# Graph attention and mixture-of-experts kernel: attention weights in a PSUM bank, two banks for the aggregates, the mask product in two halves

## The chip, the cores and the metric

The kernel runs on one core of a Trainium2 chip. The metric is device time in microseconds (us) of one execution; several executions give a median. The engines of the core are named as in the profile: PE is TensorE (matrix products; PEld are its weight loads), DVE is VectorE, ACT is ScalarE, POOL is GpSimd, SP is SyncE, which issues transfers.

## The reference

3125 nodes with 256 features, 50000 edges (src, dst, type), three layers of graph attention, then a feed-forward network of eight experts with the best two chosen per node. The part that the change touches is the message passing of a layer:

```
Q, K, V = (h @ W.T + b).reshape(-1, H, DH)  for Wq, Wk, Wv        # H = 4 heads, DH = 64
scores  = einsum('ehd,egd->ehg', Q[src], K[tgt]) / sqrt(DH)       # per edge: 4 x 4
attn    = softmax(scores, axis=-1)
msg     = einsum('ehg,egd->ehd', attn, V[tgt]) + Ee[et]
m       = segment_sum(msg @ Wo.T + bo, src)
h       = relu(layer_norm(h + m))
```

The scores of an edge are 4 by 4: each head of the source's query against each head of the target's key. The softmax runs over the four key heads, and the sum collects per source node.

## The kernel before

**Stages.** A sorting stage (to some 380 us) orders the edges by source window and scatters their records to memory; the input stage computes the first queries, keys and values; then come three times an edge phase (some 780 us each) and a node phase (some 120 us); at the end the experts.

**Edge phase.** Nodes stand in windows of 16. Edges are sorted so that a tile of 128 edges belongs to one window. Two tiles are a pair; a layer has 294 pairs (EP). A turn of the loop has 12 pairs (PAIRS): 24 full turns and one of 6 pairs per layer. The engines work side by side, each with its own program, and only semaphores order them:

- POOL gathers for each tile the 128 rows of keys and values of the edges' targets, 2 KB each, by one indirect transfer (L573, `arena<-kv_d,gidx`), two per pair, 588 per layer. The buffer `kv` holds 24 tiles, a whole turn; before POOL gathers a pair anew it waits for that pair's `agg_done` of the turn before.
- PE does for pair p, in this order: the transposes of the keys of pair p + 1 (`keys`, L1545, four) into bank 3 or 4; the aggregate of pair p - 6 (`aggregate`, L1570; LAG = 6), values times spread weights, into bank 5, 6 or 7; then `scores` of pair p into bank 0, 1 or 2. These begin with the mask product (L1553): the one-hot of the edge's node in its window, `oh[..., 1, :]`, in bf16, times a constant `maskc`, 512 columns at once, which lifts the 16 columns of the edge's own node above the others. Then follow the products of transposed keys and block-diagonal queries (L1560), which add to it. In the program an fp32 product is one call; the trace counts two instructions for it (x8 for four).
- ACT copies the transposed keys to SBUF (L1306, `kT_ready`), lays out the queries of the next pair (L1301, L1302), and copies the aggregate of pair p - 7 to `stage` in two copies (L1313, `staged`); every fourth pair it takes the exponential (L1321).
- DVE takes the largest over the 16 nodes of the window (`best`, L828), which leaves 4 by 4 scores; every fourth pair the softmax of eight tiles at once: L834 and L838, then L843, L845 and L847, which writes the normalized weights `at_s` (128x128 for eight tiles); per pair `spread` (L857): `at_s` times the one-hot `oh[..., 0, :]`, giving `att`, 128x512; and `add` (L875, two per pair), which adds `stage` to the sums of the window.
- SP loads the one-hots `oh`, one transfer for four pairs.

**Waits around the change.** `aggregate` waits for `att_ready` (the spread of its pair) and for `staged`, so that its bank has been copied out. `scores` waits for `score_read` (DVE has read the bank's earlier scores), every fourth pair for the transfer of `oh`, and, behind the mask product, for `kT_ready`. The counts of `staged` start from LAG + 3, which gives the three banks: the aggregate of a pair waits for the staging of the pair three before.

The spread, with its two operands, is

```
dve.tensor_tensor(att[...], at_s[...] (each weight for 16 nodes), oh[:, t // TG, 0, ...] (each one-hot for 16 weights), ALU.mult)
```

Of the kernel before, what the change touches and what calls it, by code (L numbers as in the profile page):

```python
# [22 lines left out]
P = 128  # L23
N, D, H, DH, E, L = 3125, 256, 4, 64, 50000, 3
# [17 lines left out]
UB = 4  # L42
# [4 lines left out]
NTURN = -(-EB // TURN)  # L47
LASTB = EB - (NTURN - 1) * TURN
TILES = TURN * UB
PAIRS = TILES // 2  # L50
# [3 lines left out]
LAG = 6  # L54
AL = LAG + 1
GP = 4
# [30 lines left out]
def build(nc, A, out):  # L87
    ctx = ExitStack()
    with ctx:
        def sb(name, shape, dt=F32):  # L90
            return ctx.enter_context(nc.sbuf_tensor(name, shape, dt))
# [15 lines left out]
        ident = sb("ident", [P, P])  # L107
# [4 lines left out]
        maskc = sb("maskc", [P, TG, DH], BF16)  # L112
# [11 lines left out]
        kv = arena[:, 0:n_kv].rearrange("p (b u n) -> p b u n", b=TURN, u=UB)  # L124
# [38 lines left out]
        ex = sb("ex", [P, 2 * GP, H, H])  # L163
        sm = sb("sm", [P, 2 * GP, H])
        rc = sb("rc", [P, 2 * GP, H])
        at_s = sb("at_s", [P, 2 * GP, H, H])
        att = sb("att", [P, 2, UB, W, H, H])

        early = arena[:, 0:n_kv]
# [46 lines left out]
        oh = sb("oh", [P, TILES // TG, 2, P], BF16)  # L216
# [98 lines left out]

        bank = [ctx.enter_context(nc.psum_tensor(f"bank{i}", [P, 512], F32)) for i in range(8)]
        bank_b = [b[:, :].bitcast(BF16) for b in bank]

        names = ("const_landed idx_landed start_ready spare wincode_ready counted place_ready perm_built perm_used "
                 "perm_done cnt_saved rec_ready wincnt_done base_ready ohwin_ready rank_ready rank_read "  # L320
# [11 lines left out]
        S = namedtuple("Semaphores", names)(*[sem(n) for n in names])  # L332
# [3 lines left out]
        gathered = [sem(f"gathered{k}") for k in range(TILES)]  # L336
        oh_landed = [sem(f"oh_landed{c}") for c in range(TILES // TG)]
# [203 lines left out]
        @block.gpsimd  # L541
        def _(pool):
            for s, k in ((S.hT_done, G), (S.q_ready, G), (S.kvp_ready, 2),
                         (S.agg_done, PAIRS), (S.score_read, 4), (S.att_ready, LAG), (S.staged, LAG + 3), (S.chain_b, AL + 2), (S.chain_a, AL)):
                pool.sem_inc(s, k)
            pool.sem_inc(S.m_y_ready, 2)
            for j in range(G):
# [4 lines left out]
            for e in range(EC):  # L552
                if e % CH == 0:
                    pool.wait_ge(S.slot_ready, e // CH + 1)
                r = P if e < EF else ER
# [123 lines left out]
        def _(dve):  # L679
# [144 lines left out]
            def e_phase(l):  # L824
# [41 lines left out]

                def add(p, u, at, q):
                    if u == 0:
                        dve.wait_ge(S.staged, at[q + 2])
                        dve.wait_ge(S.chain_b, at[q + 1])  # L870
                    else:
                        dve.wait_ge(S.chain_a, at[q])
                    w = dve.snap(wreg[2 * p + u], min_val=0, max_val=NW - 1)
                    a = acc[:, ds(w, 1), :].squeeze(1)
                    dve.tensor_tensor(a, stage[:, p % 3, u, :], a, ALU.add).then_inc(S.chain_a if u == 0 else S.chain_b, 1)  # L875
# [349 lines left out]
        def _(act):  # L1225
# [67 lines left out]
            def e_phase(l):  # L1293
# [15 lines left out]
                def sums_out(p, done, added):  # L1309
                    act.wait_ge(S.agg_done, done)  # L1310
                    act.wait_ge(S.chain_b, added)
                    for r in range(2):
                        ins = act.activation(  # L1313
                            stage[r * DH:(r + 1) * DH, p % 3].rearrange("p u (h s) -> p u h s", h=H),
                            bank[5 + p % 3][r * DH:(r + 1) * DH, 0:2 * P].rearrange("p (u g s h) -> p g u h s", u=2, g=2, h=H)[:, r],
                            ACT.Copy)
                    ins.then_inc(S.staged, 1)

# [136 lines left out]
        def _(pe):  # L1455
# [81 lines left out]
                pe.wait_ge(S.ee_ready, l + 1)  # L1537

            def e_phase(l):
                def keys(p, landed):  # L1540
                    for t in (2 * p, 2 * p + 1):
                        pe.wait_ge(gathered[t], landed)
                        for c in range(KC):
                            o = (t % 2) * D + c * P
                            ins = pe.transpose(bank[3 + p % 2][:, o:o + P], kv[:, t // UB, t % UB, c * P:(c + 1) * P], ident[:, :])  # L1545
                    ins.then_inc(S.kT_done, 1)

                def scores(p, at, here):
                    bk = bank[p % 3]
                    pe.wait_ge(S.score_read, at[p + 1])  # L1550
                    if p % 4 == 0:
                        pe.wait_ge(oh_landed[p // 4], here[p // 4 // 2])
                    mm(bk[:, :], oh[:, p // 4, 1, :],  # L1553
                       maskc[:, 2 * (p % 4):2 * (p % 4) + 2, :].unsqueeze(2).to_broadcast([P, 2, H, DH]),
                       start=True, stop=False, skip_group_check=True)
                    pe.wait_ge(S.kT_ready, at[p])
                    for u in range(2):
                        for c in range(KC):
                            o = u * D + c * P
                            ins = mm(bk[:, o:o + P], kt_s[:, p % 2, u, c, :], qbd[:, p % 4, u, :],  # L1560
                                     start=False, stop=(c == KC - 1), skip_group_check=True)
                    ins.then_inc(S.score_done, 1)

                def aggregate(p, ready):
                    pe.wait_ge(S.att_ready, ready)
                    pe.wait_ge(S.staged, ready)
                    for t in (2 * p, 2 * p + 1):
                        b, u, o = t // UB, t % UB, t % 2 * P
                        for g in range(0, H, 2):
                            ins = mm(bank[5 + p % 3][:, o:o + P], kv[:, b, u, D + g * DH:D + (g + 2) * DH],  # L1570
                                     att[:, b % 2, u, :, g:g + 2, :].rearrange("p s g h -> p g s h"),
                                     start=(g == 0), stop=(g == H - 2), skip_group_check=True)
                    ins.then_inc(S.agg_done, 1)

                def turn(i, first, last):
                    pairs = LASTP if last else PAIRS
                    at = [pe.snap(l * EP + i * PAIRS + p + 1) for p in range(pairs + 1)]
                    here = [pe.snap((l * (NTURN - h) + i + 1) * 16) for h in range(2)]
                    ahead = pe.snap((l * NTURN + i + 2) * 16)
                    for p in range(pairs):  # L1580
                        if p + 1 < pairs:
                            keys(p + 1, here[(p + 1) * 2 // PAIRS])
                        elif not last:
                            keys(0, ahead)
                        if p >= LAG or not first:
                            aggregate((p - LAG) % PAIRS, at[p])
                        scores(p, at, here)

                keys(0, pe.snap((l * NTURN + 1) * 16))
                turn(0, True, False)  # L1590
                with nc.tensor.Fori(1, NTURN - 1) as i:
                    turn(i, False, False)
                turn(NTURN - 1, False, True)
                for p in range(LAG):
                    aggregate((LASTP - LAG + p) % PAIRS, pe.snap(l * EP + EP + p + 1))
# [294 lines left out]
```

## Time and profile before

| | |
|---|---|
| time, median of 3 runs | 3674.46 us (3667.35 to 3678.6) |
| span of the profiled execution | 3674.3 us |
| PE busy | 3426.8 us, 93% of the span |
| ACT busy | 2698.7 us, 73% |
| DVE busy | 2458.4 us, 67% |
| POOL busy | 2459.9 us, 67% |
| mean granted clock of PE | 0.974 |
| edge phases, first to last gather | 516.1 to 1283, 1414.2 to 2180.7, 2311.8 to 3078.9 us |

The span is that of one execution on the chip; it lies on the median of the timed ones. The shares are averages over stages that have different limits. A busy PE is not a PE at its peak, since the ends of its products are modelled; what one product costs in a row of them is read from the starts. The pauses between two gathers of POOL count as idle, though POOL waits for nothing in them that the profile shows ("issue").

### The profile page before, as it was taken

The page shows a single profiled execution, that of the slowest core. Times are in us where ns is not written, and L with a number is a line of the kernel's source. Part 1 is how long each engine was busy: PE and PEld are TensorE (multiplying, and loading weights), DVE is VectorE, ACT ScalarE, POOL GpSimd, SP SyncE. Part 2 cuts the span into 40 slices and gives each one's busy share as a digit, 9 for nine tenths or more (in the row PEclk, how much of TensorE's full clock was granted, in tenths as well). Part 3 has the DMA queues.
Part 4 walks back from the last instruction along what each step waited for, and adds up shares of the span by engine and source line. Part 5 has one row for each costly group of instructions (what it writes and reads, how often), then busy time and mean ns, then how long its engine had stood idle before and what let it go on. Part 6 is the DMA issues. An engine that isn't in the chain of part 4 may idle for free.

```text
span 3674.3 us, 87831 instructions
## 1 busy us (share of the span) xinstructions
PE 3426.8 (93%) x25408; PEld 2968.4 (81%) x25409; DVE 2458.4 (67%) x6794; ACT 2698.7 (73%) x8426; POOL 2459.9 (67%) x2552
## 2 busy tenths in 40 slices
PE   6888879999999998999999999899999998969998
PEld 2444559999999966999999986799999997759998
DVE  7888447777777765777777775577777777931111
ACT  4999678888888856888888876788888885424443
POOL 3777127777777775777777776677777776725443
PEclk9999879999999999999999999999999999979999
DMA  2000257777777726777777753677777776446664
GB/s 80 1 1 1 90 207 205 208 208 207 207 208 206 206 94 193 205 208 207 207 206 207 208 160 115 206 206 206 209 206 207 206 207 195 155 155 182 185 176 120
DMA packets 264903, 630.75 MB, mean 172 GB/s; under 512 B 56095, under 2 KB 128726, under 8 KB 256471
## 3 DMA queue, kind: packets, MB, share of 16 engines
q0 software_dynamic: 161376, 477.59, 46.5%
q1 hardware_dynamic: 103431, 152.05, 12.4%
q8 instruction: 39, 0.64, 0.1%
q14 instruction: 57, 0.47, 0.0%
HBM read 577.72 MB, written 52.04 MB: 171 GB/s over the span
## 4 chain that ended last, share of the span: by engine, by line
PE 47%; POOL 18%; issue 17%; DMA 10%; DVE 5%; ACT 2%; DVEq 0%; POOLq 0%; SPq 0%; ACTq 0%
POOL arena L573 12%; PE bank L1570 10%; DMA arena<-kv_d,gidx 9%; PE bank L1560 8%; POOL rec_d L557 6%; PE bank L1761 5%; PE bank L1545 5%; PE bank L1773 5%; PE bank L1529 4%; PE bank L1523 2%; PE bank L1553 2%; PE bank L1605 2%; PE bank L1611 1%; DVE att L857 1%; PE bank L1683 1%
## 5 line engine op out<-in xcount | busy, mean ns | idle before, releaser
L573 POOL DMA_INDIRECT arena<-kv_d,gidx x1764 | 1763.6, 1000 | 729.1 <-issue 529.8
L1570 PE MATMUL bank<-att,arena 128*128 128x128 f32 x7056 | 946.3, 278 | 22.9 <-DVE att L857 19.4
L1560 PEld LDWEIGHTS bank<-qbd,kt_s 128*128 128x128 f32 x7056 | 932.2, 193 | 33.2
L1560 PE MATMUL bank<-qbd,kt_s 128*128 128x128 f32 x7056 | 934.8, 276 | 0.0
L1570 PEld LDWEIGHTS bank<-att,arena 128*128 128x128 f32 x7056 | 862.4, 193 | 42.0 <-DVE att L857 39.9
L828 DVE TENSOR_REDUCE sc<-bank 128x32 f32<-128x512 f32 x882 | 607.6, 689 | 313.7 <-PE bank L1560 301.7
L1306 ACT ACTIVATE kt_s<-bank 128x512 f32<-128x512 f32 x882 | 526.6, 597 | 253.3 <-PE bank L1545 239.8
L1545 PE MATMUL bank<-ident,arena 128*128 128x128 f32 x3528 | 623.4, 283 | 61.7 <-DMA arena<-kv_d,gidx 49.4
L857 DVE TENSOR_TENSOR att<-at_s,oh 128x512 f32<-128x512 f32 x882 | 608.3, 690 | 25.9
L1545 PEld LDWEIGHTS bank<-ident,arena 128*128 128x128 f32 x3528 | 407.9, 142 | 163.9 <-DMA arena<-kv_d,gidx 124.2
L875 DVE TENSOR_TENSOR arena<-stage,arena 128x64 f32 x1764 | 398.2, 226 | 196.1 <-DVE arena L875 112.4
L1301 ACT ACTIVATE qbd<-arena 64x64 f32 x1764 | 441.8, 250 | 92.6 <-issue 82.3
L1313 ACT ACTIVATE stage<-bank 64x128 f32<-64x128 f32 x1764 | 478.7, 271 | 34.6 <-DVE arena L875 10.3
L1302 ACT ACTIVATE qbd<-arena 64x64 f32 x1764 | 449.6, 255 | 20.5
L557 POOL DMA_INDIRECT rec_d<-arena x241 | 251.1, 1042 | 133.6 <-issue 78.3
L1553 PE MATMUL bank<-maskc,oh 128*128 128x512 bf16 x882 | 336.2, 381 | 0.0
L1213 DVE TENSOR_TENSOR arena<-bank,arena 128x256 f32<-128x256 f32 x56 | 23.8, 425 | 356.3 <-PE bank L1773 356.3
L658 POOL DMA_INDIRECT out<-arena,row_at x56 | 90.8, 1622 | 187.6 <-DVE arena L1217 184.6
L1761 PE MATMUL bank<-xT,arena 128*128 128x128 f32 x1792 | 210.6, 276 | 0.0
L1761 PEld LDWEIGHTS bank<-xT,arena 128*128 128x128 f32 x1792 | 205.8, 193 | 0.4 <-ACT xT L1436 0.4
L1428 ACT ACTIVATE arena<-bank,arena 128x128 f32<-128x128 f32 x448 | 121.6, 384 | 113.5 <-PE bank L1761 113.3
L1773 PE MATMUL bank<-arena 128*128 x896 | 202.6, 380 | 0.0
(246 smaller groups left out, 3999.8 us busy)
## 6 DMA issues: line engine op xcount, KB each, us to landing
arena<-in_pack SPq DMA_DIRECT2D x56, 1030.0 KB, 5.1
arena<-kv_d,gidx POOLq DMA_INDIRECT x1764, 3.7
oh<-oh_d SPq DMA_DIRECT2D x222, 64.0 KB
kv_d<-arena SPq DMA_DIRECT2D x50, 256.0 KB, 2.0
xin<-hid_d SPq DMA_DIRECT2D x75, 128.0 KB, 2.2
arena<-in_w SPq DMA_DIRECT2D x8, 1024.0 KB, 7.2
kv_d<-arena SPq DMA_DIRECT2D x5, 1280.0 KB, 5.1
hid_d<-arena SPq DMA_DIRECT2D x50, 128.0 KB, 2.0
```

The costliest lines, as they stand in the source:

```text
L557: pool.indirect_dma_start(rec_d, bass.IndirectOffsetOnAxis(slot_all[0:r, e:e + 1], 0), pay[0:r, e:e + 1], None,).then_inc(S.scattered, 16)
L573: pool.indirect_dma_start(kv[:, t // UB, t % UB, :], None, kv_d, bass.IndirectOffsetOnAxis(gidx[:, h, t - h * HT:t - h * HT + 1], 0),).the ...
L828: dve.tensor_reduce(sc[:, 2 * m:2 * m + 2], bank[q % 3][:, :].rearrange("p (t g s h) -> p t g h s", t=2, g=H, s=W), AX.X, ALU.max).then_in ...
L857: dve.tensor_tensor(att[:, b, u:u + 2].rearrange("p t s g h -> p t s (g h)"), at_s[:, 2 * m:2 * m + 2].rearrange("p t g h -> p t (g h)").u ...
L1301: act.activation(qbd[0:DH, p % 4, u, 0:64], q, ACT.Copy)
L1302: act.activation(qbd[DH:P, p % 4, u, 64:128], q, ACT.Copy)
L1306: act.activation(kt_s[:, p % 2], bank[3 + p % 2][:, :].rearrange("p (u c n) -> p u c n", u=2, n=P), ACT.Copy).then_inc(S.kT_ready, 1)
L1313: ins = act.activation(stage[r * DH:(r + 1) * DH, p % 3].rearrange("p u (h s) -> p u h s", h=H), bank[5 + p % 3][r * DH:(r + 1) * DH, 0:2 ...
L1545: ins = pe.transpose(bank[3 + p % 2][:, o:o + P], kv[:, t // UB, t % UB, c * P:(c + 1) * P], ident[:, :])
L1560: ins = mm(bk[:, o:o + P], kt_s[:, p % 2, u, c, :], qbd[:, p % 4, u, :], start=False, stop=(c == KC - 1), skip_group_check=True)
L1570: ins = mm(bank[5 + p % 3][:, o:o + P], kv[:, b, u, D + g * DH:D + (g + 2) * DH], att[:, b % 2, u, :, g:g + 2, :].rearrange("p s g h -> p ...
L1761: ins = mm(bank[1 + 2 * (p % 2) + h // 4][:, (h % 4) * P:(h % 4 + 1) * P], w1s[:, p, c * HID + h * P:c * HID + (h + 1) * P], xT[:, p % 2, ...
```

## The change

The normalized weights `at_s` no longer lie in SBUF but in PSUM, in bank 5. The aggregates use banks 6 and 7 in turn, in place of 5, 6 and 7, and the counts of `staged` start from one less, so that an aggregate waits for the staging of the pair two before; DVE's wait in `add` is shifted by the same one. `stage` keeps its three buffers. On PE, `keys` and the mask product become one function, `keys_masks`: the mask has two halves of 256 columns (one per tile), each with a weight load of its own; the first half stands behind the first transpose of the next pair's keys, the second behind the second. The waits for `score_read` and for `oh` now stand ahead of these transposes. `scores` keeps the products of keys and queries.

```diff
-        at_s = sb("at_s", [P, 2 * GP, H, H])
...
+        at_s = bank[5][:, 0:2 * GP * H * H].rearrange("p (t g h) -> p t g h", g=H, h=H)
...
-                         (S.agg_done, PAIRS), (S.score_read, 4), (S.att_ready, LAG), (S.staged, LAG + 3), (S.chain_b, AL + 2), (S.chain_a, AL)):
+                         (S.agg_done, PAIRS), (S.score_read, 4), (S.att_ready, LAG), (S.staged, LAG + 2), (S.chain_b, AL + 2), (S.chain_a, AL)):
...
-                        dve.wait_ge(S.staged, at[q + 2])
+                        dve.wait_ge(S.staged, at[q + 1])
...
-                            bank[5 + p % 3][r * DH:(r + 1) * DH, 0:2 * P].rearrange("p (u g s h) -> p g u h s", u=2, g=2, h=H)[:, r],
+                            bank[6 + p % 2][r * DH:(r + 1) * DH, 0:2 * P].rearrange("p (u g s h) -> p g u h s", u=2, g=2, h=H)[:, r],
...
+                def mask(p, u):
+                    m = 2 * (p % 4) + u
+                    mm(bank[p % 3][:, u * D:(u + 1) * D], oh[:, p // 4, 1, :],
+                       maskc[:, m:m + 1, :].to_broadcast([P, H, DH]),
+                       start=(u == 0), stop=False, skip_group_check=True)
+
+                def keys_masks(k, landed, p, at, here):
+                    if p is not None:
+                        pe.wait_ge(S.score_read, at[p + 1])
+                        if p % 4 == 0:
+                            pe.wait_ge(oh_landed[p // 4], here[p // 4 // 2])
+                    for u in range(2):
+                        if k is not None:
+                            pe.wait_ge(gathered[2 * k + u], landed)
                         for c in range(KC):
+                            if k is not None:
+                                ins = key(k, u, c)
+                            if u == 0 and p is not None:
+                                mask(p, c)
+                    if k is not None:
+                        ins.then_inc(S.kT_done, 1)
...
-                            ins = mm(bank[5 + p % 3][:, o:o + P], kv[:, b, u, D + g * DH:D + (g + 2) * DH],
+                            ins = mm(bank[6 + p % 2][:, o:o + P], kv[:, b, u, D + g * DH:D + (g + 2) * DH],
...
                         if p + 1 < pairs:
-                            keys(p + 1, here[(p + 1) * 2 // PAIRS])
+                            keys_masks(p + 1, here[(p + 1) * 2 // PAIRS], p, at, here)
                         elif not last:
-                            keys(0, ahead)
+                            keys_masks(0, ahead, p, at, here)
+                        else:
+                            keys_masks(None, None, p, at, here)
                         if p >= LAG or not first:
                             aggregate((p - LAG) % PAIRS, at[p])
-                        scores(p, at, here)
+                        scores(p, at)
```

On PE, in the body of the loop over turns, two pairs stand before the change as follows (transposes, aggregate, mask, scores; REGISTER_ALU only sets a register):

```order
L1545 MATMUL bank<-ident,arena 128x128 x4
L1570 MATMUL bank<-att,arena 128x128 x4
L1550 REGISTER_ALU
L1553 MATMUL bank<-maskc,oh 128x512
L1560 MATMUL bank<-qbd,kt_s 128x128 x4
L1545 MATMUL bank<-ident,arena 128x128 x4
L1570 MATMUL bank<-att,arena 128x128 x4
```

and after it, with the lines of the changed kernel (L1543 transpose, L1547 half a mask, L1583 aggregate, L1573 scores):

```order
L1543 MATMUL bank<-ident,arena 128x128
L1547 MATMUL bank<-maskc,oh 128x256
L1543 MATMUL bank<-ident,arena 128x128
L1547 MATMUL bank<-maskc,oh 128x256
L1543 MATMUL bank<-ident,arena 128x128 x2
L1583 MATMUL bank<-att,arena 128x128 x4
L1573 MATMUL bank<-qbd,kt_s 128x128 x4
L1553 REGISTER_ALU
```

The mask has moved from between aggregate and scores to between the first transposes of the pair, and is two instructions. On DVE nothing moves; in the softmax and the spread before the change

```order
L845 RECIPROCAL rc<-sm 128x32
L847 TENSOR_TENSOR at_s<-ex,rc 128x128
L857 TENSOR_TENSOR att<-at_s,oh 128x512
L873 ISA
L875 TENSOR_TENSOR arena<-stage,arena 128x64
```

the tile `at_s` is replaced by the bank after it:

```order
L845 RECIPROCAL rc<-sm 128x32
L847 TENSOR_TENSOR bank<-ex,rc 128x128
L857 TENSOR_TENSOR att<-bank,oh 128x512
L873 ISA
L875 TENSOR_TENSOR arena<-stage,arena 128x64
```

Only an operand of L857 and the output of L847 changed their place in memory.

## Rows read from the trace of the kernel before

**Rows 1.** Page, part 4: the chain that ended last, by line.

```profile
POOL arena L573 12%; PE bank L1570 10%; DMA arena<-kv_d,gidx 9%; PE bank L1560 8%; POOL rec_d L557 6%; PE bank L1761 5%; PE bank L1545 5%; PE bank L1773 5%; PE bank L1529 4%; PE bank L1523 2%; PE bank L1553 2%; PE bank L1605 2%; PE bank L1611 1%; DVE att L857 1%; PE bank L1683 1%
```

**Rows 2.** Stretches view, L573 alone, three edge phases summed: us, POOL busy us.

```profile
sum 2300.50, POOL 1763.60; mean POOL 587.87
```

**Rows 3.** Waits view, POOL, middle edge phase: us in total, times, longest us.

```profile
POOL arena L573 <- issue: 155.4, 510, 0.3
```

**Rows 4.** View of line L573: duration ns least/median/most, first and last start.

```profile
L573 POOL DMA_INDIRECT arena<-kv_d,gidx x1764: 942/946/1464, 516.1 to 3077.9; - x196
```

**Rows 5.** Timeline: start us, us, engine line; two gathers and the spread beside each.

```profile
552.27 0.69 DVE L857 TENSOR_TENSOR att<-at_s,oh 128x512 f32<-128x512 f32 x1
...
552.48 1.30 POOL L573 DMA_INDIRECT arena<-kv_d,gidx  x1 [0.30 <-issue]
...
3067.32 0.68 DVE L857 TENSOR_TENSOR att<-at_s,oh 128x512 f32<-128x512 f32 x1
...
3067.40 1.41 POOL L573 DMA_INDIRECT arena<-kv_d,gidx  x1 [0.30 <-issue]
```

**Rows 6.** Timeline, sorting stage: two scatters of POOL and DVE beside them.

```profile
144.07 0.36 DVE L761 CUSTOM_DVE_ANT_0 arena<-bank,arena 128x200 f32<-128x200 f32 x1
...
144.23 0.95 POOL L557 DMA_INDIRECT rec_d<-arena  x1 [0.31 <-issue]
...
145.30 0.78 DVE L750 TENSOR_TENSOR arena<-iotab,arena 128x600 bf16<-128x600 bf16 x1
...
145.49 1.42 POOL L557 DMA_INDIRECT rec_d<-arena  x1 [0.30 <-issue]
```

**Rows 7.** Groups by line and shape, DVE, experts: busy us, mean ns | idle before.

```profile
L1217 DVE TENSOR_TENSOR arena<-arena,xin 128x256 f32<-128x256 f32 x54 | 23.0, 425 | 13.3 <-DVE arena L1213 13.3
L1213 DVE TENSOR_TENSOR arena<-bank,arena 128x256 f32<-128x256 f32 x54 | 22.9, 425 | 348.1 <-PE bank L1773 348.1
```

**Rows 8.** Page, part 5: two groups of DVE in the edge phases.

```profile
L857 DVE TENSOR_TENSOR att<-at_s,oh 128x512 f32<-128x512 f32 x882 | 608.3, 690 | 25.9
L875 DVE TENSOR_TENSOR arena<-stage,arena 128x64 f32 x1764 | 398.2, 226 | 196.1 <-DVE arena L875 112.4
```

**Rows 9.** Timeline, PE, one pair and the neighbours of its start and end.

```profile
1001.62 1.06 PE L1570 MATMUL bank<-att,arena 128*128 128x128 f32 x8
1002.51 0.38 PE L1553 MATMUL bank<-maskc,oh 128*128 128x512 bf16 x1
1002.73 1.05 PE L1560 MATMUL bank<-qbd,kt_s 128*128 128x128 f32 x8
1003.62 0.60 PE L1545 MATMUL bank<-ident,arena 128*128 128x128 f32 x4
...
1004.95 0.38 PE L1553 MATMUL bank<-maskc,oh 128*128 128x512 bf16 x1
```

**Rows 10.** Timeline, ACT: the first of the two staging copies of a pair.

```profile
1003.37 0.27 ACT L1313 ACTIVATE stage<-bank 64x128 f32<-64x128 f32 x1
```

**Rows 11.** Timeline, PE: first transposes and last aggregate of the middle edge phase.

```profile
1420.35 0.66 PE L1545 MATMUL bank<-ident,arena 128*128 128x128 f32 x2 [8.26 <-DMA arena<-kv_d,gidx]
...
2197.70 1.13 PE L1570 MATMUL bank<-att,arena 128*128 128x128 f32 x8 [0.70 <-ACT stage L1313]
```

**Rows 12.** Timeline, PE: transposes directly followed by a mask.

```profile
1426.42 0.60 PE L1545 MATMUL bank<-ident,arena 128*128 128x128 f32 x4
1426.86 0.38 PE L1553 MATMUL bank<-maskc,oh 128*128 128x512 bf16 x1
```

**Rows 13.** Timeline, PE, node phase: a bf16 product of 256 columns, then fp32.

```profile
1302.37 0.28 PE L1606 MATMUL bank<-arena 18*128 18x256 bf16 x1
...
1302.58 0.48 PE L1605 MATMUL bank<-wo,arena 128*128 128x256 f32 x1
```

**Rows 14.** Waits view, middle edge phase: who waited for L857.

```profile
PEld bank L1570 <- DVE att L857: 10.9, 25, 1.7
...
PE bank L1570 <- DVE att L857: 4.3, 9, 1.5
```

More of the change, by code:

```diff
@@ L1539, in e_phase, with key, scores @@
             def e_phase(l):
-                def keys(p, landed):
-                    for t in (2 * p, 2 * p + 1):
-                        pe.wait_ge(gathered[t], landed)
-                        for c in range(KC):
[L1544 to L1548, printed above, removed]
-                    bk = bank[p % 3]
[L1550 to L1555, printed above, removed]
+                def key(p, u, c):
+                    t = 2 * p + u
+                    o = u * D + c * P
+                    return pe.transpose(bank[3 + p % 2][:, o:o + P], kv[:, t // UB, t % UB, c * P:(c + 1) * P], ident[:, :])
+                def mask(p, u):
[11 more added lines that the diff above has]
+                            pe.wait_ge(gathered[2 * k + u], landed)
+                        for c in range(KC):
+                            if k is not None:
[4 more added lines that the diff above has]
+                        ins.then_inc(S.kT_done, 1)
+                def scores(p, at):
+                    bk = bank[p % 3]
                     pe.wait_ge(S.kT_ready, at[p])
@@ L1581, in turn @@
                         if p + 1 < pairs:
-                            keys(p + 1, here[(p + 1) * 2 // PAIRS])
+                            keys_masks(p + 1, here[(p + 1) * 2 // PAIRS], p, at, here)
                         elif not last:
-                            keys(0, ahead)
+                            keys_masks(0, ahead, p, at, here)
+                        else:
+                            keys_masks(None, None, p, at, here)
                         if p >= LAG or not first:
                             aggregate((p - LAG) % PAIRS, at[p])
-                        scores(p, at, here)
-                keys(0, pe.snap((l * NTURN + 1) * 16))
+                        scores(p, at)
+                keys_masks(0, pe.snap((l * NTURN + 1) * 16), None, None, None)
                 turn(0, True, False)
```

## The prediction

> **What bounds the kernel now.** I read the chain of waits first. Its largest line is POOL's gather L573 at 12% of the span, with the landing of those gathers at 9% [rows 1]. The stretches view of the three edge phases, restricted to L573, says why: in 2300.5 us, POOL was busy for 1763.6 us with gathers alone [rows 2], and the waits view of the middle phase names as the wait before 510 of its 588 gathers "issue", never longer than 0.3 us [rows 3]. That is the pause that stands before every gather: (2300.5 - 1763.6) / 1764 = 0.304 us. So POOL never waits for a buffer: it emits 588 gathers per layer back to back, and a layer takes as long as they do, 766.8 us. The reader is to see that the engine with 93% on the page, PE, is not the bound in this stage.
>
> A gather takes 946 ns at the median, 942 at least, 1464 at most [rows 4]. If all 1764 took 946 ns they would take 1668.7 us. They take 1763.6, so 94.9 us are spent in stretched gathers. The timeline shows what stretches them. At 552.48 a gather takes 1.30 us; 0.21 us earlier DVE L857 began, and ran to 552.96. At 3067.40 one takes 1.41 us beside an L857 that began 0.08 us earlier and ran to 3068.00 [rows 5]. In both, the stretch is the end of the DVE instruction minus the gather's start, less 0.13 us (0.48 and 0.60 against stretches of 0.35 and 0.46): a fixed part of the gather does not begin before that DVE instruction is over. I went through all stretched gathers in this manner. 274 of them, from the one at 552.48 to the one at 3067.40, fit an L857 that began shortly before, and hold 90.3 us; 96 fit L838, L847 or L875 and hold 4.7.
>
> **What decides whether a DVE instruction holds POOL** is seen in the sorting stage, where other scatters run beside other DVE work [rows 6]. L750 reads two SBUF operands: the scatter at 145.49 takes 1.42 us, and 145.30 + 0.78 - 145.49 - 0.13 = 0.46 us is its stretch. L761 reads one operand from a PSUM bank and one from SBUF: it lies across the start of the scatter at 144.23 in the same way, to 144.43, and the scatter takes 0.95. So it is the second SBUF operand that holds POOL.
>
> Here a page speaks against the change. The Trainium skill, page "SBUF — State Buffer", section "Who interferes with whom", says that a VectorE instruction with two SBUF inputs contends with GpSimd's reads, but also that a probe found `tensor_tensor` not stalling DMA, and infers that descriptor generation needs only the write interface. By that inference the gathers have nothing to gain and the time stays at 3674. This trace disagrees with it: 1.42 us beside L750 and 1.41 beside L857, against 0.95.
>
> **Part 1, `at_s` in PSUM.** L857 then reads bank 5 and `oh`: one SBUF operand, the form of L761. The 274 holds go: -90.3 us. L847 writes to PSUM in place of SBUF; no DVE write to PSUM is in this trace, but L847 comes 222 times and DVE is the bound nowhere here, so I take it at nothing. What a PSUM operand costs DVE is in L1213 and L1217: the same 128x256 addition, 425 ns with one operand from a bank and 425 with both from SBUF [rows 7]. So L857 stays at its 690 ns [rows 8]. L838, L847 and L875 keep two SBUF operands, and keep their 4.7 us.
>
> **Part 2, two banks for the aggregates.** The aggregate of a pair must wait for the staging of the pair two before, not three before. Behind that wait on PE stand the scores of the same pair and all later transposes. In the loop the aggregate of a pair starts at 1001.62 [rows 9] and its two staging copies run from 1003.37 for 0.55 us (two of 0.27) [rows 10], so they end at 1003.92; the second next aggregate starts two periods of 2.44 later, at 1006.5. Slack 2.6 us: free. At a phase's end, where the last six aggregates follow one another, PE already waited 0.70 us for a staging copy [rows 11]; I allow 0 to 1 us per layer, and take 0.3, or 1 us in all.
>
> **Part 3, the mask.** A pair takes PE 2.44 us when nothing is late (1002.51 to 1004.95): aggregate 0.89, mask 0.22, scores 0.89, and the transposes the remaining 0.44 [rows 9]. The mask of 512 columns becomes two of 256, each with its own weight load, behind the first and the second transpose. A transpose followed directly by a mask costs its usual 0.11 (0.44 for four, 1426.42 to 1426.86) [rows 12], so going to bf16 is free. A half mask lasts at least half of 0.22. Coming back from it to a transpose is not in the trace with the full array. Below, the bound is 0.11, because the mask is followed by fp32 scores at 0.21 to 0.22 with nothing on top [rows 9]. Above, it is the 256-column bf16 product L1606, followed by an fp32 product after 0.21 [rows 13], 0.10 more. L1606 uses 18 rows of the array where the mask uses 128, so I take 0.11: 0.22 leave the pair in one place and 0.22 come back in another, and PE stays at 2.44. The mask's waits move ahead with it by 1.33 us (the transposes and the aggregate). The read of the bank it overwrites belongs to three pairs earlier, and the tile of `oh` is reloaded four pairs, 9.8 us, ahead; neither wait shows today, and both keep several us.
>
> **What is late next.** Without holds a gather comes every 0.946 + 0.304 = 1.25 us, 2.50 per pair. PE needs 294 x 2.44 = 717.4 us per layer, plus its waits for DVE's attention weights, 10.9 + 4.3 = 15.2 us in the middle layer [rows 14]: 732.6. From first transpose to last aggregate, the layer now takes 1420.35 to 2198.83, 778.5 us [rows 11]. Less POOL's third of 90.3 us, 30.1, this is 748.4. PE stays 15.8 us below it, so POOL is still the bound, narrowly, and the whole 90.3 us should arrive.
>
> **The sum**, against the profiled execution: 3674.3 - 90.3 + 1 = 3585. That execution lies on the median of the runs shown, 3674.46, so the forecast is 3585.
>
> **Rivals.**
> - PE pays for the switches and the kernel gets slower. With 0.10 more behind each half, a pair costs 0.20 more and a layer 58.8: 732.6 + 58.8 = 791.4 against 778.5, +12.9 per layer, 3674 + 39 = 3713. It decides from 0.156 us per pair (778.5 - 732.6 over 294), 0.078 per switch; below 0.054 per pair (15.8 over 294) it costs nothing. For it: the 0.21 of L1606 [rows 13], and that PE has so little room. Against: no row with the full array shows any of it. Chance 0.07. A smaller switch between these two points loses a part of the gain, 3590 to 3670: 0.08.
> - The change does not free POOL, because the second operand of L857 is still read by the interface that POOL needs, or a PSUM write holds it too: 3674. Against: L761 has the same operands in the same order. 0.06.
> - The holds come back through the others. With L857 gone POOL and DVE settle in a new step. L875 runs twice per pair, 226 ns [rows 8], and so can stretch a gather by at most 0.23 - 0.13 = 0.10 us; settling on about half of that once per pair gives 882 x 0.05 = 44 us, 3629. For it: two engines bound to each other keep the same step for many pairs. Against: it needs a start in a narrow span before a gather, and the three together hold 4.7 us today. 0.09.
>
> **How the numbers follow.** Forecast 3585: 0.70, with a spread of 3573 to 3600 (repeats differ by some 6 us each way, the holds that stay may be 0 or 10 us, the tail 0 to 3). Together with the returned holds at 3629 and the lower half of the partly paid switches this is about 0.82, so the range is 3573 to 3632. Faster by over 0.3% (11 us, about what a measurement of this kernel tells from no change): 0.70 + 0.08 + 0.09 = 0.87. Within 0.3%: 0.06. Slower: 0.07.
>
> **What would show it.** In the profile after: L573's mean near 949 ns in place of 1000 and POOL's phase near 737 us; no gather over 1.1 us; L857 still near 690 ns; the pair's period on PE 2.5 us, with PE waiting for gathers for about a third of what it waits now; the step from a half mask to the next transpose 0.11 us. The forecast is wrong if that step is 0.16 or more, if gathers of 1.2 to 1.4 us remain beside L857, or if POOL begins to wait for L1570, which would say that PE has become the bound.

## The result, and the profile after

The changed kernel takes 3579.98 us, the median of four runs (3577.72 to 3580.82). The kernel before took 3671.24 us beside it (3667.35 to 3678.6). The ratio is 0.9748, with a 95% interval of 0.9734 to 0.9762: 91 us faster. The forecast was 3585, the range 3573 to 3632.

The span of the profiled execution fell from 3674.3 to 3577.7 us, and POOL's busy time from 2459.9 to 2362.5; 90.1 of these 97.4 us are the gathers'. Of the 96.6 us of the span, 6.5 lie ahead of the first gather (it starts at 516.1 before and at 509.6 after), where the change touches nothing: over all the runs here that start falls between 509.0 and 516.1, and by 5 us within one kernel. First the view of their line (durations in ns as least/median/most), then two rows of page part 5, both of the kernel after; the line numbers are L573 for the gather, L857 for the spread, L1583 for the aggregate, L1573 for the scores, L1543 for the transposes and L1547 for half a mask:

```profile
L573 POOL DMA_INDIRECT arena<-kv_d,gidx x1764: 941/947/1066, 509.6 to 2980.6; - x196
```

```profile
L573 POOL DMA_INDIRECT arena<-kv_d,gidx x1764 | 1673.5, 949 | 726.6 <-issue 561.4
L857 DVE TENSOR_TENSOR att<-bank,oh 128x512 f32<-128x512 f32 x882 | 601.3, 682 | 26.0
```

The longest gather was 1464 ns [rows 4] and is 1066. Worked out as in the prediction, the stretched time is 1673.5 - 1764 x 0.946 = 4.8 us (94.9 before). None of it lies beside L857 any more.

Nor is this because the two engines have moved apart. In the timelines of the kernel before, an L857 begins at least 50 ns ahead of a gather and runs on for at least 150 ns into it 269 times, and all 269 gathers are stretched. After the change the same happens 362 times, and none of these gathers takes more than 11 ns over the median. One of them, in the position of the second gather of [rows 5] (L857 0.08 us ahead), takes 0.94 us where that one took 1.41 (timelines of DVE and POOL):

```profile
1058.34 0.69 DVE L857 TENSOR_TENSOR att<-bank,oh 128x512 f32<-128x512 f32 x1
...
1058.42 0.94 POOL L573 DMA_INDIRECT arena<-kv_d,gidx  x1 [0.30 <-issue]
```

The stretches view of the three phases, first to last gather, restricted to L573 (us, POOL busy us):

```profile
509.61:1248.95 739.34, 558.25 (x588) 0.99 0.75 219
1380.12:2116.49 736.37, 557.48 (x588) 0.99 0.75 218
2244.83:2981.51 736.68, 557.77 (x588) 0.99 0.75 216
sum 2212.39, POOL 1673.51; mean POOL 557.84
```

Against 2300.50 and 1763.60 [rows 2] this is 88.1 us less for the phases and 90.1 less for the gathers. The two differ by 2.0 us: three pauses of POOL in the first phase are longer than the usual 0.3, by 2.2 us in all. The profile puts two of them down to L1583 and one to "issue"; the longest is here (timeline, POOL):

```profile
543.16 0.94 POOL L573 DMA_INDIRECT arena<-kv_d,gidx  x1 [1.25 <-PE bank L1583]
```

In the other two phases no pause is longer than the usual 0.3, and in a second profile of the same kernel (changed_again, below) none is in any phase. The waits view of POOL in the middle phase:

```profile
POOL arena L573 <- issue: 169.1, 555, 0.3
POOL arena L573 <- PE bank L1583: 8.8, 29, 0.3
```

The second row looks like a wait for PE, but its longest is 0.3 us, the pause that stands before every gather. One with a longer figure would be a wait.

PE now runs as follows in the loop (timeline, PE):

```profile
1560.75 0.27 PE L1543 MATMUL bank<-ident,arena 128*128 128x128 f32 x1
1560.86 0.27 PE L1547 MATMUL bank<-maskc,oh 128*128 128x256 bf16 x1
1560.97 0.27 PE L1543 MATMUL bank<-ident,arena 128*128 128x128 f32 x1
1561.08 0.27 PE L1547 MATMUL bank<-maskc,oh 128*128 128x256 bf16 x1
1561.19 0.38 PE L1543 MATMUL bank<-ident,arena 128*128 128x128 f32 x2
1561.41 1.06 PE L1583 MATMUL bank<-att,arena 128*128 128x128 f32 x8
1562.30 1.06 PE L1573 MATMUL bank<-qbd,kt_s 128*128 128x128 f32 x8
1563.19 0.27 PE L1543 MATMUL bank<-ident,arena 128*128 128x128 f32 x1
```

From first transpose to first transpose it is 2.44 us, as before [rows 9]. Each of the four switches between transpose and half mask takes 0.11 us from start to start. So the switches cost nothing here.

**One view misleads here.** The chain that ended last (page part 4, by engine) now reads:

```profile
PE 66%; issue 11%; DVE 9%; POOL 9%; DVEq 2%; DMA 2%; ACT 1%; SPq 0%; POOLq 0%; ACTq 0%
```

POOL's gather, the largest line of the chain before [rows 1], is down to 3%. One could read from it that PE is the bound now. The experiments `no_mask` and `third_half` below test that.

### The profile page after: what moved, and what is told of

Read it like the earlier page. It is cut to its first block, busy times and chain, and to the rows that moved or that the text cites. A ratio compares the mean times of both kernels' runs of the same rounds, so it can differ in the third digit from the quotient of the medians.

```text
span 3577.7 us, 90206 instructions
## 1 busy us (share of the span) xinstructions
PE 3347.7 (94%) x26290; PEld 2988.5 (84%) x26291; DVE 2439.5 (68%) x6794; ACT 2701.3 (76%) x8426; POOL 2362.5 (66%) x2552
## 4 chain that ended last, share of the span: by engine, by line
PE 66%; issue 11%; DVE 9%; POOL 9%; DVEq 2%; DMA 2%; ACT 1%; SPq 0%; POOLq 0%; ACTq 0%
PE bank L1583 17%; PE bank L1573 16%; PE bank L1543 7%; POOL rec_d L557 6%; PE bank L1776 6%; PE bank L1788 5%; PE bank L1529 4%; PE bank L1547 4%; POOL arena L573 3%; PE bank L1523 2%; DVE att L857 2%; PE bank L1620 2%; DVE sc L828 1%; DVEq L865 1%; DMA arena<-kv_d,gidx 1%
## 5 line engine op out<-in xcount | busy, mean ns | idle before, releaser
L573 POOL DMA_INDIRECT arena<-kv_d,gidx x1764 | 1673.5, 949 | 726.6 <-issue 561.4
L1583 PE MATMUL bank<-att,arena 128*128 128x128 f32 x7056 | 950.5, 278 | 35.8 <-DVE att L857 31.9
L1573 PE MATMUL bank<-qbd,kt_s 128*128 128x128 f32 x7056 | 935.7, 276 | 0.0
L1583 PEld LDWEIGHTS bank<-att,arena 128*128 128x128 f32 x7056 | 861.4, 193 | 61.0 <-DVE att L857 52.4
L1573 PEld LDWEIGHTS bank<-qbd,kt_s 128*128 128x128 f32 x7056 | 862.6, 193 | 0.0
L1543 PE MATMUL bank<-ident,arena 128*128 128x128 f32 x3528 | 730.2, 275 | 36.9 <-DMA arena<-kv_d,gidx 32.7
L857 DVE TENSOR_TENSOR att<-bank,oh 128x512 f32<-128x512 f32 x882 | 601.3, 682 | 26.0
L875 DVE TENSOR_TENSOR arena<-stage,arena 128x64 f32 x1764 | 395.4, 224 | 199.0 <-DVE arena L875 115.4
L1543 PEld LDWEIGHTS bank<-ident,arena 128*128 128x128 f32 x3528 | 470.9, 142 | 68.7 <-issue 27.8
L1547 PE MATMUL bank<-maskc,oh 128*128 128x256 bf16 x1764 | 434.7, 274 | 0.0
```

The lines of the kernel that those rows point to most:

```text
L573: pool.indirect_dma_start(kv[:, t // UB, t % UB, :], None, kv_d, bass.IndirectOffsetOnAxis(gidx[:, h, t - h * HT:t - h * HT + 1], 0),).the ...
L857: dve.tensor_tensor(att[:, b, u:u + 2].rearrange("p t s g h -> p t s (g h)"), at_s[:, 2 * m:2 * m + 2].rearrange("p t g h -> p t (g h)").u ...
L1543: return pe.transpose(bank[3 + p % 2][:, o:o + P], kv[:, t // UB, t % UB, c * P:(c + 1) * P], ident[:, :])
L1547: mm(bank[p % 3][:, u * D:(u + 1) * D], oh[:, p // 4, 1, :], maskc[:, m:m + 1, :].to_broadcast([P, H, DH]), start=(u == 0), stop=False, sk ...
L1583: ins = mm(bank[6 + p % 2][:, o:o + P], kv[:, b, u, D + g * DH:D + (g + 2) * DH], att[:, b % 2, u, :, g:g + 2, :].rearrange("p s g h -> p ...
```

## The experiments

All kernels are compared with the kernel before on the same chip. "Stretched" is always the busy time of the gather's line less 1764 x 0.946 = 1668.7 us. In some executions the median gather takes 949 ns and not 946 (moved_psum, changed_again, all_softmax_again); 5 us of their figure are then no stretch.

### Each part by itself

**weights_in_sbuf**: the changed kernel without part 1.

```diff
+        at_s = sb("at_s", [P, 2 * GP, H, H])
...
-        at_s = bank[5][:, 0:2 * GP * H * H].rearrange("p (t g h) -> p t g h", g=H, h=H)
```

> The changed kernel with one part undone: the normalized weights lie in SBUF again; two banks for the aggregates and the mask in halves stay. Theory (the second SBUF operand of the spread L857 holds POOL's gathers): all holds come back, the gather's mean is 1000 ns again and the time that of before, 3671 us, within 8. Rival (the halves of the mask, which run while PE waits for the pair's second gather, or the new order of PE bring the gain): 3580 us, or at least clearly below 3650.

3716.85 us (3712.2 to 3725.6), ratio 1.0136 (1.0118 to 1.0155). Both expectations missed. The gain is gone, so part 1 is necessary to it, but the kernel is also 48 us slower than the kernel before on its chip (3668.8). The page (part 5) tells where this is:

```profile
L573 POOL DMA_INDIRECT arena<-kv_d,gidx x1764 | 1806.3, 1024 | 724.7 <-issue 532.1
```

1806.3 - 1668.7 = 137.6 us are stretched, 43 more than before. 385 gathers fit an L857 that began shortly before, in place of 274. Parts 2 and 3 thus made the holds worse, and the next runs ask which of them.

**two_banks_alone**: the kernel before with part 2 only (of each line, what changes; DVE's wait and the staging copy change with it).

```diff
-(S.staged, LAG + 3)
+(S.staged, LAG + 2)
...
-bank[5 + p % 3]
+bank[6 + p % 2]
```

> The kernel before with two banks for the aggregates in place of three and nothing else. Theory: the aggregate's wait for the staging two pairs back has 2.6 us of room in the loop and costs up to 1 us at the end of each edge phase: 3671 to 3675 us. Rival (PE stalls on staging where DVE or ACT run late at the turns of the loop): over 3682 us, with waits of L1570 for L1313 in the profile.

3673.3 us (ten runs, 3664.8 to 3678.7), ratio 1.0006 (0.9996 to 1.0015): nothing that can be told from zero. L573 takes 1763.1 us, so 94.4 are stretched, as before. The end of a phase shows a small price (timeline, last gather of the middle phase and its last aggregate):

```profile
2177.21 0.98 POOL L573 DMA_INDIRECT arena<-kv_d,gidx  x1 [0.30 <-DMA arena<-kv_d,gidx]
```

```profile
2197.80 1.13 PE L1570 MATMUL bank<-att,arena 128*128 128x128 f32 x8 [0.38 <-ACT stage L1313]
```

From 2178.19 to 2198.93 are 20.7 us; over the three layers the tail is 21.0, 20.7 and 20.1, where the kernel before has 18.7, 18.2 and 19.1: 1 to 2.5 us more each.

**halves_alone**: the kernel before with part 3 only (weights in SBUF, three banks, the mask in halves between the transposes).

> The kernel before with the mask in two halves between the transposes and nothing else: weights in SBUF, three banks. weights_in_sbuf was 46 us slower than before, with 137.6 us of stretched gathers in place of 94.9. Theory: the new order of PE alone shifts DVE's spreads against POOL's gathers, so that more of them begin just before one; then this kernel too has near 137 us of stretched gathers (L573 at 1024 ns) and takes 3715 us, within 8. Rival (it is the two banks together with the halves that make PE late): L573 near 1000 ns and 3671 us.

3720.21 us (3713.9 to 3728.6), ratio 1.0132 (1.0107 to 1.0157). The page:

```profile
L573 POOL DMA_INDIRECT arena<-kv_d,gidx x1764 | 1799.8, 1020 | 729.0 <-issue 544.1
```

131.1 us are stretched, and 127.8 of them in 364 gathers beside L857. The expectation held. So it is PE's new order that raises the holds, not the banks. DVE's program is the same as before.

**moved_sbuf**: as halves_alone, but the mask is one product of 512 columns again. It keeps the new place, behind the second transpose.

```diff
-                            if u == 0 and p is not None:
-                                mask(p, c)
+                            if u == 0 and c == 1 and p is not None:
+                                mask(p)
```

> Weights in SBUF and three banks, as in the kernel before; the mask stays one product of 512 columns, but stands behind the second transpose. Theory (the place of the mask shifts the spread against the gathers, not its halving): as with the halves alone, 3718 +- 8 us, L573's mean 1020 ns or more, over 120 us of stretched gathers. Rival (the halving does it): as the kernel before, 3671 +- 6, L573's mean 1000.

3721.13 us (3711.6 to 3726.2), ratio 1.0133 (1.0114 to 1.0152). The page:

```profile
L573 POOL DMA_INDIRECT arena<-kv_d,gidx x1764 | 1815.2, 1029 | 724.3 <-issue 550.2
```

146.5 us are stretched. The place alone does it, the halving does not: the rival (3671) falls.

### The mask's place, with the weights in PSUM

**mask_whole**: parts 1 and 2, with the mask whole and in its old place, run on two chips (the second time as **mask_whole_again**).

> The kernel before with weights in PSUM and two banks, the mask whole and in its old place between aggregate and scores. Theory: PE's pair takes 2.44 us either way and POOL is the bound, so the time is that of the changed kernel, 3580 us, within 6. Rival (the mask's new place gives part of the gain, because its 0.22 us are spent while PE waits for a gather): 3595 us or more.

> Weights in PSUM, two banks, the mask whole and in its old place, once more beside the run with the mask moved: 3590 +- 4 us if the 8 to 10 us over the changed kernel are of the kernel; 3582 or less if they were of that chip.

3590.3 us (3585.7 to 3594.1), ratio 0.9787 (0.9771 to 0.9803); then 3590.56 (3587.2 to 3592.1), ratio 0.9778 (0.9765 to 0.9792). The first expectation missed, between theory and rival; the second held: some 10 us over the changed kernel belong to the kernel.

**moved_psum**: the changed kernel, with the edit of moved_sbuf.

> The changed kernel, with the mask as one product of 512 columns behind the second transpose. Theory (the new place is what the mask's part brings): 3580 +- 4 us, L573's mean 949 ns, and PE's waits for the spread near those of the changed kernel, 84 us. Rival (the halving brings it): as with the whole mask in its old place, 3587 to 3593, and waits for the spread of some 110 us.

3577.38 us (3575.8 to 3583.8), ratio 0.9747 (0.9732 to 0.9762): as the changed kernel, on the same chip as mask_whole_again. Again it is the place and not the halving. With the weights in PSUM the new place is worth some 10 us; with them in SBUF it costs 47.

Where the 10 us lie is shown in part. mask_whole's gathers are as fast as those of the changed kernel. The pages of mask_whole, and of moved_psum:

```profile
L573 POOL DMA_INDIRECT arena<-kv_d,gidx x1764 | 1674.5, 949 | 729.0 <-issue 518.8
```

```profile
L573 POOL DMA_INDIRECT arena<-kv_d,gidx x1764 | 1676.0, 950 | 727.3 <-issue 551.2
```

But the time from the end of the last gather to the end of the last aggregate, worked out from the timelines as for two_banks_alone, is 63.6 and 65.2 us over three layers in the two runs of mask_whole, against 58.8 in the changed kernel, 56.1 in its second profile and 57.9 in moved_psum. In this tail the old place is 5 to 9 us longer. The gather phases add nothing that can be told: 2215.4 and 2213.0 us with the old place, 2212.4, 2212.8 and 2215.4 with the new one. The rest is not located. The end of the middle phase, PE's last aggregates in mask_whole_again, then in the changed kernel:

```profile
2133.39 1.16 PE L1570 MATMUL bank<-att,arena 128*128 128x128 f32 x8 [0.95 <-DVE att L857]
2136.79 6.44 PE L1570 MATMUL bank<-att,arena 128*128 128x128 f32 x40 [2.24 <-ACT stage L1313]
```

```profile
2128.35 6.66 PE L1583 MATMUL bank<-att,arena 128*128 128x128 f32 x40 [2.46 <-DVE att L857]
```

In the first, the last gather ended at 2121.09 and the last aggregate at 2143.23, 22.1 us later; in the second at 2116.49 and 2135.01, 18.5 us. Over the three layers PE also waits longer for the spread in mask_whole: 69.5 us on the page, against 52.4 in the changed kernel and 57.5 in moved_psum. These are the waits of the weight loads (PEld); the waits of the products (PE, 46.5 in mask_whole) lie within them in time and don't add to them. The rows of mask_whole, then that of the changed kernel:

```profile
L1570 PE MATMUL bank<-att,arena 128*128 128x128 f32 x7056 | 949.4, 278 | 56.3 <-DVE att L857 46.5
L1570 PEld LDWEIGHTS bank<-att,arena 128*128 128x128 f32 x7056 | 858.2, 192 | 79.9 <-DVE att L857 69.5
```

```profile
L1583 PEld LDWEIGHTS bank<-att,arena 128*128 128x128 f32 x7056 | 861.4, 193 | 61.0 <-DVE att L857 52.4
```

And PE reaches the end of a phase further behind POOL: its last scores end 8.2 to 11.4 us after the last gather in the two runs of mask_whole, and 7.2 to 8.8 in the changed kernel (two profiles) and moved_psum. That the mask, standing behind the aggregate, makes the scores wait with it for the spread is my reading; no run takes that wait apart.

### Which engine is the bound after the change

**no_mask**: the changed kernel without the mask products.

```diff
-                            if u == 0 and p is not None:
-                                mask(p, c)
...
-start=False, stop=(c == KC - 1)
+start=(u == 0 and c == 0), stop=(c == KC - 1)
```

> The changed kernel without the mask products, so a tile's scores are not restricted to the edge's own node; everything else is done as before. PE's pair falls from 2.44 to 2.22 us. Theory (POOL's gathers bound the edge phases, also after the change): POOL's phase stays at 736 us per layer, the time falls only by PE's lag at the end, 3565 to 3580 us. Rival (the chain of the changed kernel names PE with 66% of the span, so PE is the bound now): 882 times 0.22 = 194 us less, 3386 us.

3573.59 us (3570.4 to 3577.5), ratio 0.9740 (0.9724 to 0.9757), as expected of a POOL that bounds and far from the 3386 of a PE that does. PE has 0.22 us per pair less to do, 0.22 x 882 = 194 us, and the time falls by 6. PE spends what it was spared waiting for gathers (waits view, middle phase). Counted once where the two rows lie over each other, these waits are 76.0 us, 61 more than the 14.7 of the changed kernel; 294 x 0.22 = 65 were spared:

```profile
PEld bank L1543 <- DMA arena<-kv_d,gidx: 65.5, 170, 1.8
PE bank L1543 <- DMA arena<-kv_d,gidx: 29.8, 66, 7.8
```

POOL is the bound of the edge phases, whatever the chain of waits names.

**third_half**: the changed kernel with the second half of the mask issued twice, which adds 0.11 us of PE to each pair.

```diff
                                 mask(p, c)
+                                if c == 1:
+                                    mask(p, c)
```

> The changed kernel with the second half of the mask issued twice, which adds 0.11 us to PE's pair (2.55) and adds the same constant once more to scores that are already far below the others. It measures PE's room below POOL. By the sum of the prediction (PE's own time 732.6 us per layer, POOL's 748.4) 32 us more per layer pass the bound by 16: 3580 + 48 = 3628 us. With the waits for the attention weights of the profile after (17.7 + 10.0 in the middle layer) PE's own time is 745 and the time 3664. Rival (POOL has more room than that): below 3595.

3638.64 us (3634.3 to 3642.0), ratio 0.9914 (0.9898 to 0.9931). In the middle phase, the first transposes and the last aggregates (timeline, PE; the aggregate stands in L1585 here):

```profile
1404.38 0.66 PE L1543 MATMUL bank<-ident,arena 128*128 128x128 f32 x2 [8.48 <-DMA arena<-kv_d,gidx]
...
2166.24 6.62 PE L1585 MATMUL bank<-att,arena 128*128 128x128 f32 x40 [1.96 <-ACT stage L1313]
```

From 1404.38 to 2172.86 are 768.5 us. The changed kernel has 749.1, from the row below to 2135.01:

```profile
1385.89 0.66 PE L1543 MATMUL bank<-ident,arena 128*128 128x128 f32 x2 [7.90 <-DMA arena<-kv_d,gidx]
```

Of the 294 x 0.11 = 32.3 us that were added, 19.4 show: PE had 12.9 us of room in a layer; the time lies between the two expectations, nearer to that of the prediction's sum. The other one, 3664, counted PE's waits for the weights twice, in PE's row and in that of its weight loads. Counted once they are 17.7 us, PE's own time in the changed kernel is 717.4 + 17.7 = 735.1, and with 32.3 more 767.4, 1 us from the 768.5. POOL now does wait, up to 1.7 us:

```profile
POOL arena L573 <- issue: 176.1, 535, 1.7
POOL arena L573 <- PE bank L1585: 18.4, 51, 1.7
```

This is what a bound PE looks like, and the changed kernel doesn't look so.

### Freeing the other holds

**all_softmax_psum**, and on another chip **all_softmax_again**: the largest score and the reciprocal lie in bank 5 too, so that L838 and L847 also read one operand from PSUM. **changed_again** is the changed kernel once more, beside the second.

```diff
-        mx = sb("mx", [P, 2 * GP, H])
...
-        rc = sb("rc", [P, 2 * GP, H])
...
+        mx, rc = (bank[5][:, (4 + k) * 2 * GP * H:(5 + k) * 2 * GP * H].rearrange("p (t g) -> p t g", g=H) for k in range(2))
```

> The changed kernel with the largest score and the reciprocal of the sum (the second operands of L838 and L847) in bank 5 as well, so that these two have one SBUF operand. Theory: their 30 holds, 2.5 us in all, go, those of L875 (39, 1.2 us) stay; gathers over 1.01 us vanish; time 3577 us, which 3580 can't be told from. Rival (a PSUM operand makes small DVE instructions longer, and the attention weights later): L838 and L847 over 320 ns and 3585 us or more.

> The changed kernel with the largest score and the reciprocal in bank 5 too, once more. Theory (its 2.5 us of fewer holds, and no wait of POOL for PE): 2 to 8 us less than the changed kernel on the same chip. Rival (the 3573 of its first runs was the chip's or the hour's): no difference beyond 2 us.

> The changed kernel once more, beside the next one on the same chip: 3580 us.

3573.47 us (3571.4 to 3577.7), ratio 0.9741 (0.9725 to 0.9758); then 3581.82 (3579.3 to 3582.6), ratio 0.9745 (0.9729 to 0.9761), beside 3582.01 (3575.7 to 3585.3) for the changed kernel, ratio 0.9749 (0.9732 to 0.9766). The longest gather falls to 1004 ns (1009 in the second run), and of the 2.7 us that stay stretched in the first run some 1.5 lie beside L874, the addition that is L875 in the other kernels. L838 and L847 (L837 and L846 here) lie across the start of a gather 15 times in the first run and 23 in the second and stretch none; in the changed kernel that happens 23 times and each time the gather is stretched. Here it is the second operand that went to PSUM, in L857 the first: either will do. L837 takes 281 ns and L846 296, so the PSUM operand doesn't make them longer:

```profile
L572 POOL DMA_INDIRECT arena<-kv_d,gidx x1764: 942/947/1004, 509.1 to 2974.2; - x196
```

So the holds can be freed further, but on one chip the two kernels don't differ, as the rival of all_softmax_again has it, and the first run's lead came from another chip than the time it was held against. No kernel run here is measurably better than the changed one with the same work done.

### Time against stretched gathers

| kernel | place of the mask | weights | stretched us | time us |
|---|---|---|---|---|
| no_mask | none | PSUM | 1.3 | 3573.6 |
| changed | new | PSUM | 4.8 | 3580.0 |
| moved_psum | new | PSUM | 7.3 | 3577.4 |
| mask_whole | old | PSUM | 5.8 | 3590.3 |
| two_banks_alone | old | SBUF | 94.4 | 3673.3 |
| before | old | SBUF | 94.9 | 3671.2 |
| halves_alone | new | SBUF | 131.1 | 3720.2 |
| weights_in_sbuf | new | SBUF | 137.6 | 3716.9 |
| moved_sbuf | new | SBUF | 146.5 | 3721.1 |

From no_mask to moved_sbuf, 145.2 us of stretched gathers are 147.5 us of time: about one for one, in kernels with two and three banks, with the mask whole, halved and absent. halves_alone lies furthest off that line, 17 us above it, mask_whole 12 (5 to 9 of them in its tail); the stretched time is that of one execution and the time a median, and the runs come from several chips, on which the kernel before took 3669 to 3673.

## Why the prediction was right, and where its steps were not

**The bound, and the term that carries the sum: right.** The sum took 90.3 us off the gathers; 90.1 went. L573's mean was announced near 949 ns and is 949, the phase near 737 us and is 739, 736 and 737, L857 near 690 and is 682. No gather is over 1.1 us. That the second SBUF operand is what holds POOL rested on two scatters of the sorting stage [rows 6]; the runs with the weights in SBUF (131 to 147 us stretched) and in PSUM (1 to 7) show it in this place, and so do the 269 gathers of 269 that are held before and none of 362 after. The rival by which the change doesn't free POOL, 3674, falls. The inference that the Trainium skill draws on its page "SBUF — State Buffer" (section "Who interferes with whom"), that descriptor generation needs the write interface and `tensor_tensor` takes only the read one, does not carry over to these gathers. Its rule two items earlier, that a second SBUF input contends with GpSimd's reads, agrees with them. What of the gather it is that waits, no run here shows.

**PE's order: right for the switches.** A half mask followed by a transpose takes 0.11 us, the lower bound, and the pair 2.44. The rival with 0.10 for each switch, 3713, falls, and with it the one with a smaller price. The 0.10 behind L1606 [rows 13], whose product uses 18 rows of the array, doesn't carry over to a product with 128.

**Part 3 by itself: wrong, and hidden by part 1.** "0.22 leave the pair in one place and 0.22 come back in another, and PE stays at 2.44" costed the mask's new place at nothing. PE's pair did stay at 2.44, but in the kernel before PE was not the bound, and what counted was the step between DVE's L857 and POOL's gathers. The new place gave 36 to 52 us more of stretched gathers and a time 47 to 49 us longer in halves_alone and moved_sbuf. The prediction knew that the holds depend on that step (it feared them in its last rival, through L875), but it did not ask what part 3 does to it. The sum came out all the same because part 1 removes every hold of L857, however many there are: the changed kernel has 362 gathers in the place where they used to be held, more than the 269 of before. With no holds left, the same place is a gain of some 10 us, most of it in the tail, also unforeseen. How the order on PE shifts L857 against the gathers was only worked out from the trace: L857 begins 45 to 100 ns ahead of a gather 123 times before, and 185 times in halves_alone. Why it settles there stays open.

**Part 2: the tail was sized too small.** 0 to 1 us per layer was allowed and 0.3 taken. Alone it costs 1 to 2.5 us. In the sum this is covered by the mask's gain there: the tails of the changed kernel are 58.8 us in one profile and 56.1 in the other against 56.0 before, +0.1 to +2.8 where the sum had +1.

**What is late next: right, with less room.** PE was put 15.8 us per layer below POOL; third_half gives 12.9. Two errors met there. The 15.2 us of waits for the spread added two rows of the middle layer [rows 14] that lie over each other, and counted once they are 10.9, which would have made the room 20.1. And these waits did not stay as they were but rose. The rows after the change, of which the second lies within the first:

```profile
PEld bank L1583 <- DVE att L857: 17.7, 33, 2.6
PE bank L1583 <- DVE att L857: 10.0, 25, 2.5
```

With 17.7 the room is 749.1 - 717.4 - 17.7 = 14.0 us, near the 12.9.

The forecast of a PE that waits for gathers for a third of what it did came out: 40.1 us in three layers, after 147.7, 27%, counted once (the rows sum to 49.8 after 173.6). In the view of L573, those who waited for it:

```profile
  PE bank L1543: 32.7, 21
  PEld bank L1543: 17.1, 26
```

**The rival of returned holds**, 3629 through L875, falls: L875 stretches 39 gathers by 1.2 us in all, and with L838 and L847 the three hold no more than the 4.7 us of before.

**The size.** 3585 was forecast and 3580 came. The runs of before stood at 3671.2 beside it, where the sum began at 3674.3; this is 3 of the 5 us. The difference of the two medians, 91.3, is 2 more than the 89.3 of the sum. That is less than the 5 us by which the start of the first gather wanders within one kernel, so no cause is given for it. The 3674.3 was besides a span and not a time; a span is 1.8 us shorter than the time of its execution (3577.7 and 3579.51 after), so the profiled execution lay about 2 us above the median and not on it.

## What to carry to other kernels

- Where an engine emits work without pause, look at the spread of one instruction's duration before looking at its count. The distance between the median and the mean (946 and 1000 ns here), times the count, is what can be had, and the instructions beside the long ones say who holds it.
- An edit that costs its own engine nothing can still shift two others against each other. Cost a reordering with and without the hold it interacts with: the new place of the mask cost 47 us or gained 10, by where an operand of another engine lay.
- The waits of an engine's products and of its weight loads can be the same time seen twice. Lay the intervals over each other before adding the rows: here 15.2 us were 10.9.
- A chain that names an engine for 66% doesn't make it the bound. Leave work out on it, or add some, and see whether the time moves: here 194 us less gave 6, and 32 us more per layer gave 19.

## What the runs showed of the hardware

A 128x512 VectorE product with both operands in SBUF, begun just before POOL's indirect gather, stretched it from 0.95 to as much as 1.47 us. Each of the 269 gathers that such a product overlapped in this way in the kernel before was stretched, and none of the 362 with one operand in PSUM. In the kernels with the weights in PSUM and PE's work unchanged no gather took over 1.07. VectorE gave up nothing for it: L857 took 690 ns with both operands in SBUF and 682 with one in PSUM. L847, 128x128 in nearly all its calls, took 296 ns before and 304 when it wrote to PSUM. The fp32 transposes and the bf16 half masks followed one another on PE at 0.11 us each in either direction.

Not expected was how the two engines lock. The same DVE program, beside the same gathers, held POOL for 94 us in one order of PE and for 131 to 147 in another.
